# A fused four-layer kernel: seeds in PSUM for batch 0, the residual kept by VectorE, masks and identity by transfer

## The reference

```python
# L0: diffusion on the 1024 x 512 grid, reflecting edges, three scalars per batch
x = x + zX * (left - 2x + right) + zY * (above - 2x + below) + zR * x * (1 - x)
# L1: attention from one score per row; mask is prefix, postfix or "all but self" by a token of the batch
scores = tanh(x @ W1 + b1) @ v                       # W1 512 x 128
x = x + softmax(where(mask, scores, -1e30)) @ x / count
# L2: a linear layer of 8, chosen by a token of the batch
x = x + x @ weight[s].T + bias[s]                    # 512 x 512
# L3: an adapter of 8, chosen by another token, then a layer norm
y = x + relu(x @ down_w[p] + down_b[p]) @ up_w[p] + up_b[p]   # 512 -> 128 -> 512
x = x + (y - mean(y)) / sqrt(var(y) + 1e-5) * ln_g[p] + ln_b[p]
```

## Time and profile before

| what | value |
|---|---|
| timed runs | 608.26, 612.3 and 626.73 us; median 612.3 |
| profiled execution | span 618.9 us from first to last instruction; its own time is given by this span alone |
| PE, DVE, ACT, POOL busy | 574.5, 478.4, 335.5, 323.7 us |
| granted PE clock, mean | 0.964 of full |
| moved by the DMA engines | 93.84 MB, mean 152 GB/s |

### The profile page before, as it was taken

How to read it: one execution, slowest core, us unless ns; L and a number is a source line. 1 busy time by engine, 2 the same in 40 slices (tenths; PEclk the granted TensorE clock), 3 DMA queues, 4 the chain that set the end, 5 groups by cost and what they waited for, 6 DMA issues and landing times.

```text
span 618.9 us, 9325 instructions
## 1 busy us (share of the span) xinstructions
PE 574.5 (93%) x2934; PEld 441.4 (71%) x2934; DVE 478.4 (77%) x1168; ACT 335.5 (54%) x587; POOL 323.7 (52%) x279
## 2 busy tenths in 40 slices
PE   8995869999899998999899998999899998999996
PEld 2344756788659875788659885788658886688784
DVE  7536697679966998679956999679977899667456
ACT  4233457455746577465564657456664657445431
POOL 6543291368507673368516684187625684017421
PEclk8589879999999999999899999999999999999999
DMA  5576007693597457793596557892697656122362
GB/s 170 156 247 112 2 18 228 211 191 91 128 333 158 109 104 226 252 204 81 132 316 147 126 119 178 283 199 53 172 263 193 144 119 162 27 68 69 61 127 85
DMA packets 60000, 93.84 MB, mean 152 GB/s; under 512 B 10999, under 2 KB 15607, under 8 KB 59952
## 3 DMA queue, kind: packets, MB, share of 16 engines
q0 software_dynamic: 16544, 29.90, 29.6%
q1 hardware_dynamic: 34192, 46.58, 22.6%
q10 hardware_dynamic: 9216, 16.78, 7.4%
HBM read 61.26 MB, written 31.98 MB: 151 GB/s over the span
## 4 chain that ended last, share of the span: by engine, by line
PE 50%; DVE 37%; issue 7%; ACT 5%; POOL 1%; DMA 1%; SPq 0%; DVEq 0%; ACTq 0%; POOLq 0%
PE y L636 16%; DVE x2f L1451 9%; DVE xd L1316 6%; PE front_ps L672 6%; DVE xu L1284 6%; PE front_ps L695 5%; DVE x L1323 4%; DVE o_sb L1483 4%; PE front_ps L750 3%; PE front_ps L648 3%; DVE wtl L1418 2%; PE front_ps L680 2%; PE front_ps L686 2%; DVE stats L1467 2%; PE front_ps L636 2%
## 5 line engine op out<-in xcount | busy, mean ns | idle before, releaser
L533 POOL TENSOR_TENSOR norm<-norm 128x1 f32<-128x1 f32 x64 | 37.8, 591 | 187.2 <-DVE norm L1478 187.2
L636 PE MATMUL y<-wth,x2h 128*128 128x512 f32 x256 | 103.7, 405 | 10.6 <-DVE wtl L1418 10.6
L551 POOL TENSOR_TENSOR x2l<-x2f,x2h 128x1024 fp32r<-128x1024 f32 x32 | 81.9, 2561 | 45.6 <-ACT x2h L923 31.4
L636 PE MATMUL y<-wth,x2l 128*128 128x512 f32 x256 | 101.0, 395 | 0.0
L636 PE MATMUL y<-wtl,x2h 128*128 128x512 f32 x256 | 100.4, 392 | 0.0
L540 POOL DMA_DIRECT2D out<-o_sb x58 | 68.4, 1214 | 13.8 <-ACT o_sb L1054 10.5
L1467 DVE BATCH_NORM_STATS2 stats<-y 128x6 f32<-128x512 f32 x64 | 44.3, 692 | 39.3 <-PE y L636 39.3
L509 POOL TENSOR_TENSOR xd<-xn 128x1024 f32<-128x1024 f32 x28 | 61.7, 2206 | 24.7 <-DVE x L1323 16.6
L1451 DVE SCALAR_TENSOR_TENSOR x2f<-alb,small,front_ps 128x128 f32<-128x128 f32 x256 | 70.2, 337 | 2.2 <-POOL x2l L551 0.4
L750 PE MATMUL front_ps<-th_pt,x 128*128 128x129 f32 x512 | 68.2, 281 | 2.8 <-DVE x2f L1451 1.8
L750 PEld LDWEIGHTS front_ps<-th_pt,x 128*128 128x128 f32 x512 | 63.7, 191 | 9.3 <-DVE x2f L1451 6.2
(11 more groups left out here) (148 smaller groups left out, 1184.9 us busy)
## 6 DMA issues: line engine op xcount, KB each, us to landing
xn<-in_x SPq DMA_DIRECT2D x32, 512.0 KB, 11.3
out<-x ACTq DMA_DIRECT2D x58, 256.0 KB, 4.4
out<-o_sb POOLq DMA_DIRECT2D x58, 256.0 KB, 5.5
xu<-in_x SPq DMA_DIRECT2D x21, 512.0 KB, 11.0
xu<-in_x POOLq DMA_DIRECT2D x21, 512.0 KB, 7.6
wn<-in_L_cond_weight SPq DMA_DIRECT2D x8, 1024.0 KB, 5.4
wd<-in_L_cond_down_w SPq DMA_DIRECT2D x8, 256.0 KB, 5.3
wu<-in_L_cond_up_w SPq DMA_DIRECT2D x8, 256.0 KB, 4.1
```

What stands on the lines that cost most here:

```text
L551: pool.tensor_tensor(x2l[q][:, k, :], x2f[:, k % 2, :], x2h[q][:, k, :].bitcast(F32), ALU.subtract).then_inc(x2l_ready, 1)
L636: ins = mm(dst, lhs, rhs, start=first and q == 0, stop=last and q == len(parts) - 1, skip_group_check=True)
```

## The change

- **Batch 0's diffusion.** ACT squares x (`square`), DVE adds left + right (`add_sides`), ACT writes zX times that into a PSUM bank as its seed (`seed_rows`; four `fill` matmuls on zeros prepare the banks), and PE adds one fp32 product with zY above and below plus the centre on the diagonals (`sides`), and one fp32r product for the edge rows, split in two parts. DVE finishes with one operation per block (`first_diffuse`).
- **Biases.** The three bias rows are loaded as 128 x 512 broadcasts. POOL makes `start_row` = L2 bias + up_b (`start_sum`) and `rest_row` = ln_b - up_b (`rest_difference`). ACT seeds all 8 banks with `start_row`. DVE makes x3 = bank + `rest_row` (`keep_x3` moves from ACT to DVE). The products with `rows_on`, `spread_bias`, `keep_bias`, `round_bias` and `bias_rest` are gone. The three y banks now rotate over batches (`bank(b, t)`).
- **Mask and identity.** SP loads the mask from `masks` by token (`load_mask`), and POOL adds the identity to the weights by an accumulating transfer (`add_identity`). The scalars are read from `table` directly.
- **Orders.** `program` becomes `opening`, `first`, `steady` and `last` on every engine, each with a new order.

The core of the diff (the new orders cut to VectorE's and to the places that the prediction speaks of):

```diff
+            def load_mask(n):
+                kind = token(itok_B_0_2, n, 3)
+                sp.wait_ge(const_made, 2)
+                wait_past(sp, al_ready, n)
+                sp.dma_start(mask[:, :], masks[:, bass.ds(kind, 1), :].rearrange("p o m -> p (o m)")
+                             ).then_inc(mask_loaded, 16)
...
+            def steady(b, n, m, q):                          # SP
+                if m is not None:
+                    load_mask(m)
+                    load_linear(m)
+                    load_rows(m)
+                    load_next(m, 3)
+                    load_next(m, 1)
+                    load_next(m, 0)
+                    load_next(m, 2)
+                    load_scale(m)
...
+            def start_sum(n):
+                pool.wait_ge(row_loaded, 48 * n + 48)
+                row = start_row[:, n % 2, :]
+                pool.tensor_tensor(row, row, up_row[:, :], ALU.add).then_inc(start_ready, 1)
+            def add_identity(n):
+                if n == 0:
+                    pool.wait_ge(const_made, 1)
+                pool.wait_ge(wt_loaded, 64 * n + 64)
+                pool.dma_start(w_diagonal, ident[:, :].rearrange("p (o h) -> p o h", o=1).to_broadcast([P, KD, P]),
+                               accum_op=ALU.add).then_inc(wn_ready, 16)
...
+                root(b, 7)                                   # end of POOL's steady
+                finish(b, 7)
+                root(n, 0)
+                if m is not None:
+                    add_identity(m)
+                finish(b, 6)
...
-                mm(y[:, :], rows_on[:, 1, :], bias[:, q, :], start=False, stop=False, skip_group_check=True)
...
+                mm(row_ps[t], sides, xn[:, t // 2, t % 2, 1:D + 1], start=False, stop=False, skip_group_check=True)
+                if t == 0:
+                    pe.wait_ge(ends_ready, 1)
+                    pe.wait_ge(edges_split, 2)
+                mm(row_ps[t], ends[:, t, :], edge_parts, start=False, stop=True, skip_group_check=True
...
+                adapter_up(n, q, 0)                          # PE's steady, the scores
+                if m is not None:
+                    spread_scores(m, 0)
+                    score_hidden(m, 1 - q, 1)
+                adapter_up(n, q, 1)
+                if m is not None:
+                    spread_scores(m, 1)
+                    scores_by_row(m)
+                    down_through_w(m)
+                    block_sums(m)
...
+            def seed_rows(c):
+                act.wait_ge(sides_added, c + 1)
+                act.wait_ge(rows_filled, min(2 * c + 2, 4))
+                wait_past(act, l0_done, c - 1)
+                for j in range(2):
+                    act.activation(row_ps[2 * c + j], xd[:, c % 2, j, :], ACT.Identity,
+                                   scale=scalar(Z_X, 0)).then_inc(rows_seeded, 1)
+            def seed(b, t):
+                act.wait_ge(start_ready, b + 1)
+                if NJ * b + t < YB:
+                    act.wait_ge(rows_taken, NJ)
+                else:
+                    act.wait_ge(y_free, NJ * b + t - YB + 1)
+                copy(bank(b, t)[:, :], start_row[:, b % 2, :]).then_inc(y_seeded, 1)
...
+            def keep_x3(b, t):                               # DVE
+                dve.wait_ge(rest_ready, b + 1)
+                dve.wait_ge(y_ps, NJ * b + t + 1)
+                if b == LAST and t - XB >= FIRST_LAST:
+                    dve.wait_ge(last_sum, t - XB - FIRST_LAST + 1)
+                else:
+                    dve.wait_ge(base_stored[t % XB], 16 * (NJ // XB * b + t // XB) + 16)
+                dve.tensor_tensor(x3[:, t % XB, :], bank(b, t)[:, :], rest_row[:, b % 2, :],
+                                  ALU.add).then_inc(x3_ready, 1)
...
+            def steady(b, n, m, q):                          # DVE
+                maxima(n)
+                block_weights(n)
+                row_weights(n)
+                probabilities(n, 0)
+                rest_v(n)
+                keep_x3(b, 2)
+                moments(b, 1)
+                adapter_bias(n)
+                probabilities(n, 1)
+                keep_x3(b, 3)
+                subtract_mean(b, 1 - q, 1)
+                moments(b, 2)
+                moments(b, 3)
+                subtract_mean(b, 1 - q, 2)
+                carry_products(n, 0)
+                carry_sums(n, 0)
+                add_carry(n, 0, 2)
+                if m is not None:
+                    add_around(m, 0)
+                keep_x3(b, 4)
...
+                    times_x(m, 3)
+                    diffuse(m, 1 - q, 3)
+                keep_x3(n, 0)
+                rest_z(n, 0)
+                moments(n, 0)
+                if m is not None:
+                    mask_scores(m, 0)
+                keep_x3(n, 1)
+                subtract_mean(n, q, 0)
+                rest_z(n, 1)
+                if m is not None:
+                    mask_scores(m, 1)
```

More of the change, by code:

```diff
@@ L296, in blk, with run, scalar @@
             return slice(j * P, (j + 1) * P)
-        def run(eng, program):
-            program(None, None, 0, 1)
-            program(None, 0, 1, 0)
-            for i in range(B - 2):
-                program(i, i + 1, i + 2, 1 - i % 2)
-            program(B - 2, B - 1, None, 1)
-            program(B - 1, None, None, 0)
+        def run(opening, first, steady, last):
+            opening()
+            first()
+            for b in range(B - 2):
+                steady(b, b + 1, b + 2, 1 - b % 2)
+            steady(B - 2, B - 1, None, 1)
+            last()
+        def scalar(which, n):
+            return table[:, which, n:n + 1]
         block = ctx.enter_context(nc.Block())
@@ L438, in _, with last @@
+            def last():
+                pass
+            run(opening, first, steady, last)
         @block.gpsimd
@@ new lines, in first @@
+            def first():
+                rest_up(0, 0)
+                add_below(1, 0)
+                add_below(1, 3)
+                add_below(1, 1)
+                add_below(1, 2)
+                left_and_right(1, 0)
+                left_and_right(1, 1)
+                rest_difference(0)
+                start_sum(0)
+                rest_x2(0, 0, 0)
+                rest_x2(0, 0, 1)
+                rest_x2(0, 0, 2)
+                rest_x2(0, 0, 3)
+                left_and_right(1, 2)
+                left_and_right(1, 3)
+                root(0, 0)
+                add_identity(1)
@@ L625, in _ @@
             diagonals()
-            run(pool, program)
+            run(opening, first, steady, last)
         @block.tensor
@@ new lines, in opening @@
+            def opening():
+                fill(ys[0][:, :])
+                fill(ys[1][:, :])
+                fill(ys[2][:, :])
+                fill(cbank)
+                sum_rows(0)
+                sum_rows(1)
+                sum_rows(2)
+                sum_rows(3)
+                transpose_x1(0, 0, 0)
+                sum_rows(4)
+                sum_rows(5)
+                transpose_x1(0, 0, 1)
+                sum_rows(6)
+                sum_rows(7)
+                transpose_x1(0, 0, 2)
+                score_hidden(0, 0, 0)
+                transpose_x1(0, 0, 3)
+                score_hidden(0, 0, 1)
+                spread_scores(0, 0)
+                spread_scores(0, 1)
+                scores_by_row(0)
+                down_through_w(0)
+                block_sums(0)
+                transpose_p(0, 0)
@@ new lines, in steady @@
+            def steady(b, n, m, q):
+                small_exps(n)
+                row_exps(n)
+                round_v(n)
+                keep_p(n, 0)
+                store_base(b, 2)
+                store_base(b, 3)
+                keep_p(n, 1)
+                scale(b, 1)
+                if m is not None:
+                    reflect(m, 0)
+                keep_alpha(n)
+                seed(b, 4)
+                if m is not None:
+                    scale_rows(m, 0)
+                scale(b, 2)
+                store_base(b, 4)
+                seed(b, 5)
+                if m is not None:
@@ L1209, in _, with last @@
+                seed(n, 3)
+            def last():
+                scale(LAST, 1)
+                seed(LAST, 4)
+                seed(LAST, 5)
+                seed(LAST, 6)
+                seed(LAST, 7)
+                store_last(2)
+                store_last(3)
+                store_last(5)
+                store_last(6)
+                store_last(4)
+                store_last(7)
+            run(opening, first, steady, last)
             for q in range(OB):
@@ L1619, in _ @@
             make_table()
-            run(dve, program)
+            run(opening, first, steady, last)
 _INS = ["x", "condB_zX", "condB_zY", "condB_zR", "itok_B_0_2", "itok_B_0_7", "itok_B_0_6",
```

1109 lines of the change are left out of this document (525 added, 584 removed).

## The result

The changed kernel takes 643.71 us (median of four runs, 640.16 to 648.85); the kernel before took 610.28 us beside it (four runs, 604.66 to 626.73). The ratio is 1.0566, with a 95% interval of 1.0474 to 1.0659: 33 us slower, where 17 us faster was forecast. Of the stated outcomes the nearest is the rival that had 12%, the identity that lands late (626 us), and the time lies 18 us beyond it. Twenty of the 66 timed executions of the kernel before took 617 to 629 us, at a mean granted clock of 0.950 to 0.970 where it was recorded, and are left out of the ratios; the profile that the prediction used (618.9 us, 0.964) looks like one of them.

A forecast was written before the change was run, and what follows sets the result against it. A steady batch was taken as bound by VectorE for 44 us and TensorE for 26. Steady steps -3.5, opening -6, first stage -4 and last stage -3.5 gave -17 from 612.3: 595 us, range 580 to 612.

The forecast's parts named there:

- The identity by transfer: Ahead of down_through_w: GpSimd's transfer lands between 250.8 and 257.5 us, mostly before 254.5; +0.6 us a step.
- Rival 3: Identity lands late ahead of down_through_w: 5 us a batch, seven times, +31, 626 us; chance 12%.
- SP's new order: x loads wait for the last diffuse at 245 us; channels were full until 255 before too, so price 0.
- The base: Savings summed against the profiled span of 618.9 us, then the same saving subtracted from the median of 612.3.
- The opening: Batch 0's row sums: cheaper second product against a later first sum; net -9 or -3 by the clock, taken as -6.
- near 32 us: Sign that the forecast holds: the first score_hidden starts near 32 us, where the profile read had 37.92.
- The first stage: 47 to 112 us: left_and_right runs earlier, away from the softmax's slow VectorE operations, and bias matmuls go; -4 us.
- The steady steps without the identity: Each steady batch: bias matmuls -0.9, VectorE's stretch +0.5, scores -0.8 us; the identity's +0.6 left out.
- ring: A steady batch has 44 us paced by VectorE and 26 by TensorE; a term counts only where its engine is late.
- +0.5 for keep_x3: VectorE's 44 us stretch: four keep_x3 +2.4, both rest_z out -1.2, subtract_mean of block 2 out -0.7 us.
- rival 1: TensorE is the bound everywhere after the new orders: all 2.8 us a batch count, 582 us, steps of 67.5; chance 22%.
- The last stage: From 537.22 to 603.40 us: 18 bias matmuls worth 4.1 us, less 0.6 for the tail's later x3; -3.5.

The follow-up runs named there:

- e1: The changed kernel with the identity added by VectorE ahead of the scores' masks instead of by GpSimd's transfer; 607.74 us, ratio to before 0.9949.
- e4: The changed kernel with SyncE issuing the next batch's x loads only after the identity has landed; 627.78 us, ratio 1.0268.
- e3: The kernel before with only the identity's transfer by GpSimd, behind root(n, 0), put in; 646.82 us, ratio 1.0586.
- e5: The kernel before, unchanged, profiled once more; 607.78 us, span 606.0.
- e9: Identity on VectorE as in e1, plus seven zero products on TensorE ahead of the first row sum; 601.75 us, ratio 0.9894.
- e2: The changed kernel with the identity's transfer issued earlier, behind root(b, 7) and ahead of the x loads; 611.47 us, ratio 0.9987.
- e12: The opening of e10 and the last batch of e11 together; 598.75 us, ratio to the kernel before 0.9832.
- e7: e1 with an extra VectorE sum of 304 columns beside each keep_x3, eight a batch; 614.79 us, ratio 1.0061.
- e6: e1 with one extra matmul on zeros in each adapter_up, eight a batch; 613.1 us, ratio 1.0038.
- e10: e9 with edges loaded before x's second chunk, seeds before edge scaling, and side products of two blocks first; 603.18 us, ratio 0.9877.
- e8: e1 with x3 of the last batch's blocks 2 to 7 copied by ScalarE and rest_row added by GpSimd; 605.64 us, ratio 0.9924.
- e11: e1 with the last batch's blocks 2 to 7 the old way: both biases seeded, ScalarE copies, one TensorE product each; 605.45 us, ratio 0.993.

## Why the prediction was wrong

1. **The identity by transfer, +0.6 a step (bounds 0 to about 5).** This is the step that failed. The prediction took the landing to lie mostly before 254.5, that is within 5.6 us of the end of root at 248.94, "since the size is 256 KB but both ends are on chip". Measured: 8.3 to 11.8 us from issue to landing, stalls of 2.2 to 5.6 us (4.5 on the average) and some 2 us more for down_through_w at the lower clock; against e1 a step is 6.5 us longer (74.7 against 68.2), beyond the upper bound too, 39 us in six. The size and the ends are not what makes it late, as e4 shows: 4.0 us without the x loads. What shares the channels with it matters, and the prediction had the row for it in hand (share 1.06 in just that stretch) and the nearest row too (7.5 us for 256 KB under load), and chose the other end. Rival 3 had the mechanism and the place right; its price, 5 us a batch, lacked the clock, and it stood on a forecast that was too low without it as well: e1 has no such transfer and takes 607.7 us.
2. **SP's new order, price 0.** This term is not what failed: with the old order the transfer is as late (e3, 9.4 to 10.6 us from issue to landing) and the loss as large. What failed is that "full until 255 too" was read for the x loads alone. Full channels cost TensorE nothing while it waits for no transfer among them; in a steady step the identity is the first one that it waits for.
3. **The base.** 618.9 us held 13.6 us in opening and first stage that the second profile does not have (e5). The same saving was then subtracted from a median that did not hold them.
4. **The opening, -6 (-9 or -3 by the clock).** Measured in score_hidden: 33.27 us after and 32.65 in e1, against 26.68, so +6 to +6.6. Held against the 37.92 that it read, 33.27 looks nearly like the sign that it named ("near 32 us"); that is luck, since 37.92 held 11 us of its own. The sums do get shorter (1.4 to 1.5 us each in e9, for 2.1), but the first starts at 13.7 us in place of 7, 6.7 us later where +3 was taken (ScalarE waits for the edges until 11.7), and the 6 us pause costs half clock, 4.4 us (e9).
5. **The first stage, -4.** Measured: from block_sums of batch 0 to that of batch 1 63.8 us in e1, against 62.0 in the kernel before again: +1.8. The lock in the softmax that was to be avoided is not in the softmax of the second profile of before, and the new order meets it there: in e1 one 128x64 operation of VectorE's takes 2.31 us, beside GpSimd's left + right (0.22 us in e5). In the changed kernel, e2, e9 and e12 one small operation there takes 2.7 to 2.9 us. First the row of the chain, then GpSimd's:

```profile
46.59 2.31 DVE small L1438
...
46.92 4.70 POOL L542 TENSOR_TENSOR xd<-xn 128x1024 f32<-128x1024 f32 x1
```

ScalarE's exponentials and the rest of the softmax stand behind it, and TensorE waits 5.28 us for them, against 3.49 in e5. The clock falls behind the wait in both, in e1 for longer (0.50 from 56 to 60 us; in e5 0.61 and 0.53 from 48 to 52). How the 1.8 us divide over the lock and the clock was not tested.

```profile
55.92 1.08 PE L784 MATMUL front_ps<-ident,pn 128*128 128x128 f32 x4 [5.28 <-DVE bz L1493]
```

6. **The steady steps without the identity, -1.2.** The direction held and the size was too small: -2.3 (70.47 to 68.2). A steady batch of e1, to be held against the 66.96 and 58.63 of the earlier trace rows:

```profile
251.11:319.12 68.01, 64.89 (x353) 51.42 (x352) 58.02 (x146) 39.03 (x69) 42.46 (x33) 1.00 0.75 180
```

TensorE 2.07 less, VectorE 0.61 less though it has eight keep_x3 more. keep_x3 took 0.68 us, as predicted. But the ring of "44 us paced by VectorE and 26 us paced by TensorE" does not describe the new orders: there VectorE's added work counts for a tenth (e7), so the +0.5 for keep_x3 was hardly paid, and TensorE's for a half to three quarters (e6), where the forecast let a third of the twelve products count. At e6's rate the twelve are worth 1.4 to 2.1 of the 2.3 us (an estimate from 0.9 to 1.4 us for eight). The step of 68.2 us lies nearer to the sign of rival 1 (67.5) than to the forecast's (69.8): the new orders leave TensorE as the bound for most of a step. Whether the ring described the kernel before was not tested.
7. **The last stage, -3.5.** Measured +5.4 in e1. The same code of the last batch takes 84.5 us where the clock stays full (e2) and 87.0 to 88.6 where it falls once or twice (e1, e9, the changed kernel, e4, e10), so some 2.5 of e1's 5.4 us are the clock. With VectorE's six sums taken away, six products given back and the clock full it is 83.0 (e12): 1.5 us. The other 1.3 against the 81.7 of before are left. TensorE stands still there for 2.6 us and then for 1.85 us, the second time for a keep_x3 of VectorE's (e2); the kernel before has only 1.2 us. So what eighteen products fewer may be worth went under in the waits of the new order and the clock behind them. The prediction read the earlier trace rows (TensorE 64.88 of 66.18) and did not ask whether VectorE, at 39.73, was dense at the end of the stretch, nor what a new wait of TensorE's would cost in clock.

## What to carry to other kernels

A transfer that replaces a cheap instruction must be priced by what is on the channels when it is issued, not by its size: look for the row of the channels' share at its place, and issue it ahead of the bulk loads or not at all. A pause of TensorE can cost more than its length, since the clock may fall: products of zeros in a pause of 6 us won 4.4 us back. Extra work put on one engine at a time (e6, e7), read stage by stage, tells which engine is the bound where; the total alone did not. And before stages are costed, a second profile of the kernel before tells which slow stretches are its own and which belong to one execution.

## What the runs showed of the hardware

- The same accumulating transfer of 256 KB within SBUF (512-byte pieces) landed in 4.0 us without the x loads (e4), in 8.1 issued 2.5 us ahead of them (e2) and in 8.3 to 11.8 us among 4 MB of them.
- The granted clock fell with each of TensorE's six waits of 2.2 to 5.6 us for the identity (down_through_w 5.28 to 6.79 us in place of 3.68). In the last stage the same two pauses, 2.6 us and 1.85 us, left it full in e2, e8 and e12, and it fell once in e1 and e9 and twice in the changed kernel, e4, e10 and e11. In the opening of the kernel before it fell to half in one execution, some 5 us after a pause of 1.0 us, and not in another that had no such pause: 11.2 us of difference at score_hidden (37.92 against 26.68).
- A VectorE instruction with two SBUF inputs went from 0.75 to 1.64 us beside a GpSimd sum of 1.28 us (e8); a 128x64 operation from 0.22 to 2.31 us beside left + right (e1); a 128x7 copy on VectorE took 5.63 us in the profile of e5 while GpSimd made left + right:

```profile
48.55 5.63 DVE L1266 COPY cur<-table 128x7 f32<-128x7 f32 x1
```
